# A recurrent layer with residual: sums of weights, biases and x moved from VectorE into accumulating DMAs, and biases multiplied out of a single row

## The reference

```python
xW = jnp.einsum('ntd,dg->ntg', x, Wx) + b          # x: (32, 512, 512), Wx: (512, 2048)
def step(carry, xw_t):
    prev_h, prev_c = carry
    a = xw_t + prev_h @ Wh                         # Wh: (512, 2048)
    i, f, o = (jax.nn.sigmoid(a[:, k*Hd:(k+1)*Hd]) for k in range(3))
    g = jnp.tanh(a[:, 3*Hd:])
    next_c = f * prev_c + i * g
    next_h = o * jnp.tanh(next_c)
    return ((next_h, next_c), next_h)
# scan over 512 steps from h0 = cond, c0 = 0
return x + swapaxes(hs, 0, 1)
```

## Time and profile before

| | |
|---|---|
| median of three runs | 2547.26 us (2546.9 to 2547.31) |
| profiled execution, from first to last instruction | 2545.2 us |
| TensorE busy | 2524.4 us (99%) |
| VectorE busy | 2034.3 us (80%) |
| ScalarE busy | 1556.6 us (61%) |
| GpSimd busy | 47.2 us (2%) |
| DMA | 109.79 MB, mean 43 GB/s |

### The profile page before, as it was taken

How to read it: one execution, slowest core, us unless ns; L and a number is a source line. 1 busy time by engine, 2 the same in 40 slices (tenths; PEclk the granted TensorE clock), 3 DMA queues, 4 the chain that set the end, 5 groups by cost and what they waited for, 6 DMA issues and landing times.

```text
span 2545.2 us, 162019 instructions
## 1 busy us (share of the span) xinstructions
PE 2524.4 (99%) x67268; PEld 1805.6 (71%) x67268; DVE 2034.3 (80%) x8604; ACT 1556.6 (61%) x5895; POOL 47.2 (2%) x132
## 2 busy tenths in 40 slices
PE   8999999999999999999999999999999999999998
PEld 2677777777777777777777777777777777777775
DVE  7887888788788878887888788878887888788876
ACT  7666666666666666666666666666666666666664
POOL 0000000000000000000000000000000000000000
PEclk9999999999999999999999999999999999999999
DMA  4111111111111111111111111111111111111100
GB/s 172 39 45 37 37 41 45 37 37 42 45 37 40 41 43 37 41 43 40 37 41 45 37 37 41 45 37 37 41 45 37 37 41 45 37 37 41 45 33 27
DMA packets 56925, 109.79 MB, mean 43 GB/s; under 512 B 6336, under 2 KB 6720, under 8 KB 55872
## 3 DMA queue, kind: packets, MB, share of 16 engines
q1 hardware_dynamic: 56816, 109.37, 12.6%
q10 hardware_dynamic: 80, 0.03, 0.0%
HBM read 75.83 MB, written 33.55 MB: 43 GB/s over the span
## 4 chain that ended last, share of the span: by engine, by line
PE 96%; DVE 2%; DMA 1%; ACT 0%; issue 0%; SPq 0%; POOL 0%; DVEq 0%
PE Z L376 71%; PE run L376 19%; PE extra L376 6%; DMA wh_raw<-in_Wh 1%; DVE wx_lo L924 0%; DVE wh_lo L929 0%; DVE h_hi L988 0%; ACT tanh_c L629 0%; DVE gc L1005 0%; DVE hT_hi L993 0%; SPq L300 0%; DVE h_lo L1028 0%; ACT wx_hi L640 0%; DVE igfc L999 0%; DVE gc L1014 0%
## 5 line engine op out<-in xcount | busy, mean ns | idle before, releaser
L376 PE MATMUL Z<-wh_hi,hT_hi 128*32 128x512 f16 x8176 | 795.5, 379 | 8.7 <-DVE hT_hi L993 8.7
L376 PE MATMUL Z<-wh_lo,hT_hi 128*32 128x512 f16 x8176 | 795.8, 379 | 1.1 <-DVE wh_lo L929 1.1
L618 ACT ACTIVATE act<-Z 128x128 f32<-128x128 f32 x1024 | 287.5, 281 | 566.2 <-PE Z L376 566.2
L376 PE MATMUL Z<-wh_hi,hT_lo 128*32 128x512 f16 x8176 | 529.9, 379 | 0.0
L629 ACT ACTIVATE tanh_c<-gc 128x64 f32<-128x64 f32 x1024 | 262.6, 256 | 315.5 <-DVE gc L1014 248.9
L376 PE MATMUL run<-wx_hi,x_hi 128*32 128x256 f16 x6048 | 427.5, 273 | 3.3 <-DVE x_lo L781 2.3
L376 PE MATMUL Z<-wx_hi,x_hi 128*32 128x256 f16 x6048 | 427.4, 273 | 0.2 <-DVE wx_lo L924 0.2
L376 PE MATMUL Z<-wx_lo,x_hi 128*32 128x256 f16 x6048 | 427.5, 273 | 0.0
L376 PE MATMUL run<-wx_lo,x_hi 128*32 128x256 f16 x6048 | 427.5, 273 | 0.0
L376 PE MATMUL Z<-wx_hi,x_lo 128*32 128x256 f16 x6048 | 427.4, 273 | 0.0
L376 PE MATMUL run<-wx_hi,x_lo 128*32 128x256 f16 x6048 | 427.4, 273 | 0.0
(11 more groups left out here) (120 smaller groups left out, 3961.5 us busy)
## 6 DMA issues: line engine op xcount, KB each, us to landing
x_res<-in_x_rows SPq DMA_DIRECT2D x128, 256.0 KB, 2.7
out_y<-y SPq DMA_DIRECT2D x127, 256.0 KB, 2.0
x_T<-in_x_cols SPq DMA_DIRECT2D x126, 256.0 KB, 2.6
wx_raw<-in_Wx SPq DMA_DIRECT2D x4, 1024.0 KB, 12.8
wh_raw<-in_Wh SPq DMA_DIRECT2D x4, 1024.0 KB, 13.4
y<-in_x_cols SPq DMA_DIRECT2D x2, 256.0 KB, 6.3
bias_bc<-in_bias_rows SPq DMA_DIRECT2D x1, 256.0 KB, 16.3
out_y<-y SPq DMA_DIRECT2D x1, 192.0 KB, 1.9
```

The lines of the kernel that those rows point to most:

```text
L376: return nc.tensor.matmul(out, lhsT, rhs, start=False, stop=last, skip_group_check=True)
L618: nc.scalar.activation(half_gates(act, a)[:, 0:2], half_gates(Z[s], a)[:, 0:2], ACT.Sigmoid, scale=scale).then_inc(gates_done, 1)
```

## The change

- **T1 to T4 of the second chunks** (cp = 1) are no longer made on VectorE. SyncE loads one summand, GpSimd issues a DMA that adds the other (add_w): t3[:,1], t1[:,1]; then t1[:,0] (which holds T2) is a copy of t3[:,1] within SBUF with a part of Wx added, and t3[:,0] (T4) is a part of Wx to which t1[:,0] is added. SyncE waits for wx_lo_cut and t3_added among its first loads; GpSimd for each summand and for t2_added.
- **Signs.** A DMA can add but not subtract, so the scheme's signs are moved: T1, T3 and T4 are sums, S1 a difference and S4 a sum, set_c12 copies with scale -1.0, and the last addition of add_extra is a subtraction.
- **Bias of the differences**, bias_d, becomes a sum made by such a DMA.
- **x plus h.** h is written into y[:, r, s] (h32 is gone), and for all blocks but the last a DMA issued by GpSimd at the end of the block adds x to y; SyncE waits for it (x_added) before it stores. x_res is gone. The last block is added on VectorE (add_x_last), with x loaded into x_raw in the last block but one.
- **Bias of the raw steps** is multiplied from one row: `one` (1 x 32) with `bias_row` (1 x 4 x 512), which ScalarE's queue loads first of all. Four of the eight bias sets open the banks Z, one stands before the third chunk of Wx, three before the first recurrent part. The five extra rounds of opening matmuls and `pick` are gone.
- **Loads.** x of the raw steps goes to x_raw; h0 is loaded ahead of Wh.

```diff
+            for b in Z:
                 for j in range(NJ):
+                    mm = nc.tensor.matmul(b[L * j:L * j + B, :], one[:, :], bias_row[:, j, :], start=True, stop=True)
+                mm.then_inc(banks_opened, 1)
...
             def rest_of_raw(s):
-                bias_part(s)
                 for ch in WX_ARRIVE[2:]:
                     mm = raw_x_part(s, ch)
                 mm.then_inc(raw_summed, 1)
...
-            bias_part(0)
+            bias_part(TB)
             pe.wait_ge(wx_loaded[WX_ARRIVE[2]], 16)
             raw_x_part(0, WX_ARRIVE[2])
-            bias_part(1)
...
+            for s in range(1, TB + 1):
                 rest_of_raw(s)
+            for s in range(TB + 1, 2 * TB):
+                bias_part(s)
```

On SyncE, after the loads of x for blocks 2 and 3:

```diff
-            load_res(0, 0)
+            sp.dma_start(t3[:, 1], Wx[3][:, HG:]).then_inc(t3_loaded, 16)
+            sp.dma_start(t1[:, 1], Wx[1][:, HG:]).then_inc(t1_loaded, 16)
+            sp.dma_start(bias_d[:, :], bias_rows[:, HW:]).then_inc(bias_d_loaded, 16)
+            sp.wait_ge(wx_lo_cut, CUT[W_NAMED["T3"], 0] + 1)
+            sp.dma_start(t3[:, 0], Wx[3][:, 0:HG]).then_inc(t4_loaded, 16)
+            sp.wait_ge(wx_lo_cut, CUT[W_NAMED["T1"], 0] + 1)
+            sp.wait_ge(t3_added, 16)
+            sp.dma_start(t1[:, 0], t3[:, 1]).then_inc(t2_loaded, 16)
...
-                    sp.wait_ge(y_done, n * TB + TB)
+                    sp.wait_ge(x_added[r], i * 16 + 16)
                     sp.dma_start(flat(out[n]), flat(y[:, r])).then_inc(y_stored[r], 16)
```

On GpSimd:

```diff
+            def add_w(made, loaded, given, added):
+                pool.wait_ge(loaded, 16)
+                nc.gpsimd.dma_start(made, given, accum_op=ALU.add).then_inc(added, 16)
+
             share_wmax(0)
+            add_w(t3[:, 1], t3_loaded, Wx[1][:, HG:], t3_added)
+            add_w(t1[:, 1], t1_loaded, Wx[1][:, 0:HG], t1_added)
+            add_w(bias_d[:, :], bias_d_loaded, bias_rows[:, 0:HW], bias_d_done)
+            add_w(t1[:, 0], t2_loaded, Wx[1][:, 0:HG], t2_added)
             share_wmax(1)
             share_xmax(2, 0)
+            pool.wait_ge(t2_added, 16)
+            add_w(t3[:, 0], t4_loaded, t1[:, 0], t4_added)
+
+            def add_x(i, n, r):
+                pool.wait_ge(h_lo_done, n * TB + TB)
+                nc.gpsimd.dma_start(flat(y[:, r]), flat(x_rows[n]), accum_op=ALU.add).then_inc(x_added[r], 16)
```

On VectorE, in prepare, hidden and block:

```diff
-                make_t1(1)
                 cut_wx_lo(0, "B22")
-                make_t3(1)
                 cut_wh_lo(0)
...
                         scale_block(2, 0)
-                        make_t2(1)
                     if first(n) and s == 2:
-                        v.wait_ge(bias_loaded, 16)
-                        nc.vector.tensor_tensor(bias_d[:, :], bias_bc[:, HW:], bias_bc[:, 0:HW], ALU.subtract).then_inc(bias_d_done, 1)
...
                             cut_wx_lo(1, "T3", "B22")
-                            make_t4(1)
...
-                    add_x(i, s, r)
+                    if isinstance(n, int) and n == NB - 1:
+                        add_x_last(s, r)
```

On ScalarE:

```diff
-                nc.scalar.copy(Z[2 * e][:, HW:], run[e][:, 0:HW]).then_inc(c12_set, 1)
+                nc.scalar.activation(Z[2 * e][:, HW:], run[e][:, 0:HW], ACT.Copy, scale=-1.0).then_inc(c12_set, 1)
```

More of the change, by code:

```diff
@@ L72, in lstm_residual @@
         bias_d = sb("bias_d", [P, HW])
-        pick = sb("pick", [P, NJ, B])
+        one = sb("one", [1, B])
         x_abs = sb("x_abs", [P, 2, TB * C], F16)
@@ L379, in _ @@
             pe.wait_ge(zeros_set, 2)
-            for b in Z + run + extra:
+            for b in run + extra:
                 for j in range(NJ):
@@ L637, in cut_wx_hi @@
                     made = {"T1": t1_made, "T2": t2_made, "T3": t3_made, "T4": t4_made}.get(name)
-                    if made is not None:
-                        sc.wait_ge(made, cp + 1)
+                    added = {"T1": t1_added, "T2": t2_added, "T3": t3_added, "T4": t4_added}.get(name)
+                    if cp == 0 and made is not None:
+                        sc.wait_ge(made, 1)
+                    if cp == 1 and added is not None:
+                        sc.wait_ge(added, 16)
                     nc.scalar.activation(wx_hi[:, k, cp], w_form(k, cp), ACT.Copy, scale=row_scale(cp)).then_inc(wx_hi_cut, 1)
@@ L896, in make_t2, with make_t1 @@
[L896 to L918, removed]
+            def make_t1():
+                v.wait_ge(wx_loaded[0], 16)
+                nc.vector.tensor_tensor(t1[:, 0], w_block(0, 1)[:, 0], w_block(0, 0)[:, 0], ALU.add).then_inc(t1_made, 1)
@@ new lines, in make_t3, with make_t2 @@
+            def make_t3():
+                v.wait_ge(wx_loaded[2], 16)
+                nc.vector.tensor_tensor(t3[:, 0], w_block(1, 1)[:, 0], w_block(0, 1)[:, 0], ALU.add).then_inc(t3_made, 1)
+            def make_t2():
+                v.wait_ge(t1_made, 1)
+                v.wait_ge(t3_made, 1)
+                v.wait_ge(raw_done, 1)
+                v.wait_ge(wx_summed, 1)
+                nc.vector.tensor_tensor(w_form(W_NAMED["T2"], 0), t3[:, 0], w_block(0, 0)[:, 0], ALU.add).then_inc(t2_made, 1)
@@ L920, in cut_wx_lo, with make_t4 @@
+            def make_t4():
+                v.wait_ge(t2_made, 1)
+                v.wait_ge(raw_done, 2)
+                v.wait_ge(wx_lo_cut, CUT[W_NAMED["B21"], 0] + 1)
+                nc.vector.tensor_tensor(w_form(W_NAMED["T4"], 0), w_block(1, 0)[:, 0], w_form(W_NAMED["T2"], 0),
+                                        ALU.add).then_inc(t4_made, 1)
             def cut_wx_lo(cp, *forms_cut):
@@ L932, in constant_tables @@
             def constant_tables():
[L933 to L936, removed]
+                nc.vector.memset(one[:, :], 1.0).then_inc(one_set, 1)
                 nc.vector.memset(wx_sum[:, 0, 3:4], 2.0 ** (LOW_FIELD - EXP_ONE)).then_inc(least_set, 1)
@@ L960, in prepare @@
                 set_h_scale(0, 0)
-                make_t1(0)
+                make_t1()
                 sum_of_last_half(2, 0)
                 scale_of_rows(0)
-                make_t3(0)
+                make_t3()
                 cut_wx_lo(0, "B11")
-                make_t2(0)
+                make_t2()
                 cut_wx_lo(0, "B21", "T1", "T2")
                 sum_of_last_wh()
-                make_t4(0)
+                make_t4()
                 largest_weight(0)
@@ L979, in prepare @@
                 cut_wh_lo(1)
-                hidden(0)
+                hidden(0, 0, 0, 0)
                 cut_wh_lo(2)
@@ L1036, in hidden, with step @@
                     turn_high_part(t, a)
-                low_part_of_h(t)
-            def step(t):
+                low_part_of_h(t, i, s, r)
+            def step(t, i, s, r):
                 if isinstance(t, int) and t == T - 1:
@@ L1068, in block @@
                     if not first(n) or s > 0:
-                        step(n * TB + s)
-                    if first(n) and s == 0:
-                        v.wait_ge(raw_summed, TB - 1)
+                        step(n * TB + s, i, s, r)
                     if first(n) and s == 1:
@@ L1150, in block @@
                     share_xmax(n + 3, 1 - r)
+                if within(n + 1, NB):
+                    add_x(i, n, r)
             run_blocks(pool, block)
```

99 lines of the change are left out of this document (47 added, 52 removed).

## The result

The changed kernel takes 2552.58 us (median of 15 runs, 2549.92 to 2554.26), the kernel before 2547.31 us (15 runs beside them, 2546.89 to 2547.61): a ratio of 1.0021, 95% interval 1.0015 to 1.0028. It is slower by 5.3 us, where I had forecast a gain of 4.2. The profiled execution's span is 2550.5 us, 5.3 above that of before.

A forecast was written before the change was run, and what follows sets the result against it. Bound by TensorE's pace in steady steps and VectorE's chain at the start; 1.5 + 0.20 + 0.24 + 0.51 + 0.20 + 1.33 + 0.20 = 4.2 us off 2547.3 gave 2543.1 us, range 2541.0 to 2551.0.

The forecast's parts named there:

- the 4.2 of VectorE's chain: At the start, 20 to 82 us: sums and additions taken off VectorE free 4.2 us of its chain.
- The price is the opening: TensorE's opening: one-row biases start raw x at about 7.0, hidden up to 7.8, so cost 0.
- is there at about 3: Opening: the 8 KB bias row, issued in the first microsecond, lands at about 3 us, from a 32 KB store's 2.1.
- The pace: Opening: four bias sets take 3.4 us at full pace, plus 0.5 if half pace lasts to about 4.
- At half pace throughout: Opening's worst case: bias sets all at half pace, raw x starts at 9.9, costing some 2 us.
- So TensorE gives nothing there: Late bias sets, before the first recurrent part: hidden by the wait for wh_lo and VectorE's chain, so 0.
- the second, biases not hidden in the loads: Rival in the opening: half pace or a late row costs 1 to 2 us, 2544.1 to 2545.1; chance 0.12.
- T2 was not late: Rival at ScalarE's cut of T2's second chunk: T2 comes 6.5 us late at A = 12, 2549.6; chance 0.10.
- A: Time of one 512 KB accumulating DMA in T2's path: taken as 5 us, cost 0 up to 8.7.
- The pieces didn't come free whole: Rival on VectorE's starting chain: all pieces come free whole, 6.1 us, giving 2541.2; chance 0.14.
- GpSimd's descriptors held up nothing: Rival at each block's end: descriptor writing stalls VectorE; at 1.0 us it costs 45, giving 2588; chance 0.12.
- make_t2 and the addition: VectorE's starting chain before the forms: 1.42 us removed, only about 0.24 free, the rest waiting for ScalarE's scaled x.

The follow-up runs named there:

- experiment 1: The changed kernel with TensorE's part undone (zeros open all banks, five extra rounds, 128-row biases at their old places), all sums by DMA kept: 2543.38 us, 0.9985 of the kernel before.
- experiment 8: The changed kernel with the bias row's load moved from ScalarE's queue to the head of SyncE's: 2549.68 us, 1.0009 of the kernel before.
- experiment 3: The changed kernel with its order of work, but biases multiplied over 128 rows (pick and bias_bc, loaded first on ScalarE's queue): 2547.66 us, 1.0002 of the kernel before.
- experiment 4: The changed kernel with 13 rounds of zero matmuls over 128 rows ahead of the one-row bias sets: 2550.68 us, 1.0012 of the kernel before.
- experiment 2: As experiment 1, but the bias sets multiply one row, at the old places: 2544.3 us, 0.999 of the kernel before.
- experiment 6: The kernel before with TensorE's part of the change alone, its sums staying on VectorE: 2554.9 us, 1.003 of the kernel before.
- experiment 7: The changed kernel with the three late one-row bias sets back inside steps 5 to 7, the opening still changed: 2551.85 us, 1.0019 of the kernel before.

## Why the prediction was wrong

**Where the 9.2 us lie.** I compare the changed kernel with experiment 1 at the end of the first recurrent part, 49.11 and 40.04, 9.07 us apart. Raw x starts at 13.07 for 6.87: 6.20, of which the late row is 2.8 (experiment 8) and the half pace 7.05 - 3.6 = 3.4. Raw x's first four sets take 5.71 for 3.80: 1.9. One set less stands ahead of the first recurrent part: -0.86. The recurrent part takes 4.04 (45.07 to 49.11) for 2.85 (37.19 to 40.04): 1.2. That makes 8.4. The other 0.6 lie in the sets of one row, which take 0.99 for 0.86, the last one more, at a falling clock (0.46 together), and in the two products of 128 rows that stand right ahead of such sets (3.54 for 3.43 and 1.83 for 1.72 us, 0.2 together). Against before, the 4.2 of VectorE's chain come off: 9.4 - 4.2 = 5.2 by the pieces at 96.52, 87.14 and 91.31.

**The step that failed** is the one that the prediction put as "The price is the opening", with "I take 0". It held a start of raw x at 7.0, a limit of 7.8 up to which it is hidden, and a start of 9.9, some 2 us, as its worst. The start was 13.07. Two terms of it were wrong:
- The row "is there at about 3". I had taken a lone store of 32 KB, 2.1 us, as the price. The 8 KB landed at 5.95, 5.08 us after the DMA began on ScalarE's queue, beside the loads of weights on SyncE's; issued ahead of those on SyncE's queue, it was there before 3.26. The nearest row was one of an empty machine; the rows of the opening would have said more.
- The pace. I let the half pace of the openings end at about 4, as it does for 128 rows. With one row it didn't end, and it went on into raw x. "At half pace throughout" was in my rival, but priced with a row that comes at 3 and with a raw x at full pace.

**"So TensorE gives nothing there"** failed with it. It had two grounds, that the first recurrent part waits for wh_lo anyway and that the rests of later steps lie in VectorE's shadow. The first was gone once TensorE was 6 us late: its recurrent part began at 45.07, the cuts of wh_lo ended at 46.87, and it took them up at 48.25 without a wait. And in this trace the clock fell while the last of three sets of one row ran (0.80 from 44 to 45), so that the part behind them took 4.04 us; in experiment 8 it didn't, and the part took 2.60. Here experiment 3 shows what the places cost without the row: 4.3 us, which is the start of raw x, 12.00 - 6.87 = 5.1, less the one set of 0.86.

**The rivals.** Closest was the second, biases not hidden in the loads, with its mechanism right for the opening and its price wrong: 1 to 2 us where it was 9.2; the fall of the clock behind the late sets wasn't in it. It should have been the one that ends slower than before. T2 was not late, though in experiment 1 the copy took 6.3 us for the 3.3 that I gave it and A 5.7 to 5.9, for the 5 that I took and the 3.2 of the estimate beside it; where they differ, the measurement holds. (The upper end of the range, 2551.0, was not worked out right: A of 13 gives 2543.1 + 8.5 = 2551.6. The measured time lies above both.) The pieces didn't come free whole: 4.17 in the trace of experiment 1 for the 4.2 of the sum, 3.7 by medians, not 6.1. And GpSimd's descriptors held up nothing: 127 DMAs that add, the first of which took GpSimd 0.88 us in experiment 1, left TensorE's waits at 3.6 us. By the rule of the Trainium skill (SBUF — State Buffer, "Who interferes with whom") that I had set beside that rival, a VectorE instruction with two SBUF inputs contends with a GpSimd instruction that reads SBUF, not with one that only writes it. The trace agrees as far as it goes: the first product of a step, igfc, takes 226 ns in the mean of 512 in both kernels.

**What held.** The steady steps at 0, ScalarE's scaled copy at 0, the loads and SyncE's waits at 0, and VectorE's chain piece by piece, within 0.3 us at each of the four places compared under experiment 1. Between the forms and wx_lo my sum had 0.24 for make_t2 and the addition, though the times it names give 48.26 - 47.88 = 0.38; the trace has 2.00 - 1.44 - 0.31 (the difference of biases) = 0.25. What I said would show it wrong, "raw x beginning later than 7.8", is what showed it.

**The spread.** The 15 runs of the changed kernel lie 4.3 us apart, those of experiments 4 and 8 5.1 and 4.2, those of experiments 2 and 6 2.0 and 2.4, while experiments 1 and 3 keep within 0.8 and the kernel before within 0.8, 0.8 and 1.2 in its three sets of runs. The mean granted clock, on record for every run, goes with it: in experiment 4 the five runs under 2550 us have 0.999 and the five over 2551 have 0.998; in experiment 2 the two runs at 2545.9 have 0.999 and the eight others 1.000; in the changed kernel the fastest run has 1.000 and the slowest 0.997, and so in experiment 8. A mean lower by 0.001 over 2550 us is 5.1 us at the 0.50 level, which do the work of 2.55, so it costs some 2.5 us (an estimate from these records). So the spread goes with how much clock a run lost. Where a run lost it only profiled executions show, and experiment 7, whose clock falls too, keeps within 1.0; that the late sets make the difference from run to run is argued, not shown.

**Open.** In experiments 3, 6, 7 and 8 the clock fell once more between 64 and 76 us, after stretches with TensorE partly idle. In experiment 3 these are 128-row products throughout:

```profile
62.00:64.00 2.00, 0.84 (x24) 0.55 (x24) 1.72 (x7) 1.66 (x8) 0.00 (x0) 1.00 0.73 123
...
66.00:68.00 2.00, 2.00 (x27) 0.86 (x20) 2.00 (x3) 2.00 (x5) 0.00 (x0) 0.50 0.03 9
```

In the changed kernel and in experiment 1 it didn't fall there, though TensorE was busy for 2.80 of 5 us at 65 to 70 in the one and 3.18 of 5 at 55 to 60 in the other. Why it fell in some and not in others I leave open, as I do why it fell behind the late sets in three traces of four. It cost experiment 3 some 0.65 us, the 4.16 by which it was behind experiment 1 at the end of the first recurrent part against 4.81 at the later piece.

**The better kernel** is experiment 1: all sums by DMA, biases as they were. It beats both, by 0.15% and 0.36%.

## What to carry to other kernels

A sum that fills idle DMA queues is a good trade where its deadline can be worked out from a chain, and its price should be taken from a DMA under the same load, not from one on an empty machine. Matmuls over one row cost no less time than over 128. Four sets of them in the opening neither brought TensorE's clock up nor held it, in all five traces that had them, and three in a row let it fall in three traces of four: put them singly between large ones, or multiply them out over 128 rows, and not first in a kernel or several together ahead of the part that sets the pace. When the first thing that TensorE does is made to wait for a load, every wait that used to hide it further on must be counted again from the new start.

## What the runs showed of the hardware

- Sixteen float32 matmuls of 512 columns over one row stayed at half pace for 7.05 us without a gap (experiment 8), and took the clock from the 1.00 to the 0.50 level where they began at full pace (experiment 4); the same over 128 rows came up to full pace within 5.43 us (experiment 3). At the full clock sixteen of either in a row take the same time, 3.63 us over one row (experiment 4) and 3.61 over 128 (experiment 3); a single set of four between products of 128 rows takes 1.00 for 0.86 (experiment 2). The Trainium skill (TensorE: Matmul & The Clock Gate, "Why this matters for your kernels") says that a single matmul over 32 rows takes the time of one over 128. For one row these traces agree while the clock is full, but for the 0.14 us of a lone set.
- Three sets of one row left the clock at 1.00 in experiment 8 and were followed by 0.50 in the changed kernel and in experiments 4 and 6.
- The record of the granted clock reads 1.00 in the first 10 us of every trace here, while matmuls there start at half pace (sixteen in float16 take 1.68 us from start to start at 1.21 and 0.86 later). In these traces the pace, not the record, tells of a kernel's start.
- Beside the first loads of weights, 8 KB loaded on ScalarE's queue landed after 5.08 us and 256 KB in its place after 5.8 (experiment 3), so the time of the row was hardly one of its bytes.
- DMAs that add, issued by GpSimd, in the changed kernel: 256 KB from HBM 4.1 us (a plain load 2.7), 512 KB from HBM 5.9, 512 KB within SBUF 4.8, and the plain copy of 512 KB within SBUF, issued by SyncE, 6.5. In the other kernels that have them the last three are 5.7 to 7.8, 4.8 to 6.0 and 4.3 to 6.4, so they depend on what runs beside them.
